# A blockwise scan with one exact iteration a block instead of two

## Chip, cores, metric

One core of a Trainium2 chip runs the kernel. The metric is the device time of one execution in microseconds (us); the times of the kernel before are the median of three runs and the profile of one more execution.

## What is computed

The input x is 2 sequences of 1024 rows of 128 numbers. Three residual layers follow each other: half a mixture of experts (a shared feed-forward layer and the best two of 8 experts), then a layer that learns while it reads, then half the same mixture again. The change is in the middle one:

```python
k, v = split(layernorm(x) @ W_KV)             # time first: 1024 steps, 2 rows each
def loss_fn(params, k_t, v_t):
    return mean((silu(k_t @ W1 + b1) @ W2 + b2 - v_t) ** 2)
def step(params, kvt):
    g = grad(loss_fn)(params, *kvt)
    return params - LR * g, None               # LR = 0.001, for each of W1, b1, W2, b2
params, _ = scan(step, (W1, b1, W2, b2), (k, v))
out = mlp(params, x @ W_Q)
```

So there are 1024 gradient steps, each on the parameters that the one before left.

## The kernel before, in words

The steps are taken in 16 blocks of 64 steps, 128 rows each (one row for each step and sequence). Within a block the activations of all 128 rows are guessed from the parameters at the block's start and the corrections that the earlier rows of the block make; the guess is put back in and the products are taken again. One such pass over a block is called an iteration here: h (`pe_first`, plus `pe_again`, L1050, which adds the correction by the old d), a silu and a tanh on ScalarE (ACT), y and the inner product a·a masked to earlier rows (`pe_y`, `pe_aa`, `dve_aa`, `pe_inner`), e on VectorE (DVE, `dve_e`), dA on TensorE (PE, `pe_da_old`, `pe_da`), the slope of silu on GpSimd (POOL, `pool_slope`) and d = slope times dA on DVE (`dve_d`). The rows of e and d then give the sums that move W1, b1, W2 and b2 (`pe_w1_sums` and its siblings, `moved_by` on DVE).

Two chains of iterations run side by side. The chain `ahead` is rounded: its operands are of type fp32r, and one product is one matmul record. The chain `final` is exact fp32, and one product is two records; a transposition is one in either. They have four banks of PSUM each, their own semaphores and their own copies of the parameters.

The scan is a loop of 16 turns, written out in full for each engine (the loops `for turn in range(NBLK)`). In turn t the exact chain does two iterations on block t (`late[0]` from the last rounded iteration, `late[1]` from `late[0]`), takes the sums and moves the exact parameters. The rounded chain meanwhile does two iterations (`early[0]`, `early[1]`) on block t+1; its parameters are the exact ones after block t-1 plus its own sums of block t. In the last turn there is no rounded chain. The order in which each engine issues these operations is laid down by hand in five loops (PE, ACT, DVE, POOL, and the helpers); every engine works its queue in order, and the semaphores release it.

POOL also measures how far the two exact iterations differ (`gap`, L1497), squares and adds that, and squares and adds the last iteration itself. After the last turn DVE reduces the sums (L1820), PE adds them over the partitions, and DVE compares with the tolerance TOL. The result is a flag: at 0 all engines run 1024 single steps instead (`If(ok == 0)`). In the profiled execution that branch was not run. The products for the queries x @ W_Q stand on PE before and behind the sum of the squares.

Of the kernel before, what the change touches and what calls it, by code (L numbers as in the profile page):

```python
# [42 lines left out]
ROUNDS = 2  # L43
# [12 lines left out]
TOL = 5e-5  # L56
# [6 lines left out]
class Chain:  # L63
# [39 lines left out]
    ee_mm: Any  # L103
# [7 lines left out]
class Step:  # L111
# [9 lines left out]
    inner: bool = True  # L121


def mk_macaron(nc, x, wq, wkv, w1, b1, w2, w2t, b2, router, experts, out):
# [20 lines left out]
    with ExitStack() as ctx:  # L145
# [6 lines left out]
        def sem(name):  # L152
# [110 lines left out]
        last_ed = sb("last_ed", [P, ROUNDS, 2, P])  # L263
        last_aa, last_ee = (sb(n, [P, 2, P]) for n in ("last_aa", "last_ee"))
        b1_half = sb("b1_half", [P, 1])
        gap, gap_sq, new_sq = (relu[:, n // 2, n % 2 * 2 * P:(n % 2 + 1) * 2 * P].rearrange("p (a d) -> p a d", d=P)
                               for n in range(3))
        squares = y_out[:, 0:4, :]
        slots_dram = [nc.dram_tensor(f"slots_dram{f}", (NT * P, ROW), F32) for f in range(2)]
        y_dram = nc.dram_tensor("y_dram", (TOPK * T, P), F32)  # L270
        norms = sb("norms", [P, 4])
        nrm = sb("nrm", [1, 4])
        good = sb("good", [1, 2])
# [68 lines left out]
        new_squared = sem("new_squared")  # L342
        gap_done = sem("gap_done")
# [29 lines left out]
        def chain_sems(name, own):  # L373
# [12 lines left out]
                      rows_done=None, ee_mm=None, **chain_sems("ahead", ()))  # L386
# [3 lines left out]
                      w2t_sb[:], b1_sb[:], b1_half[:], b2_sb[:], **chain_sems("final", ("rows_done", "ee_mm")))  # L390
# [579 lines left out]
        def pool_key_part(pool, part, g):  # L970
# [10 lines left out]
            elif part == 4:  # L981
# [5 lines left out]
        PARAMS = ("w1", "b1_half", "b1", "b2", "w2t", "w2", "ahead_w1", "ahead_b1_half", "ahead_b1", "ahead_b2",  # L987
                  "ahead_w2t", "ahead_w2")
        LAST_PARAMS = ("w1", "b1_half", "b1", "b2", "w2t", "w2")
# [26 lines left out]
        def turn_steps(turn):  # L1016
# [34 lines left out]
        def pe_again(pe, step):  # L1051
# [3 lines left out]
            mm(x.h_bank, old.chain.ed[:, old.to, 1, :], old.chain.kk[:, step.block, :], start=False)\  # L1055
# [36 lines left out]
        def pe_aa(pe, step, turn):  # L1092
# [4 lines left out]
            if x is final and step.m:  # L1097
                pe.wait_ge(x.ee_done, step.m)
            if x is final:
                wait_param(pe, step, turn, "b1")  # L1100
# [14 lines left out]

        def pe_y_old(pe, step):

            x, old = step.chain, step.old
            pe.wait_ge(x.ee_done, old.m + 1)
            pe.wait_ge(x.erows_done, old.n + 1)  # L1120
            mm(x.y_bank, x.ed[:, old.to, 0, :], x.aa[:, old.to, :], stop=False)
            pe.wait_ge(x.a_done, step.n + 1)

        def pe_y_last(pe, step):
            x = step.chain
            mm(x.y_bank, x.w2, x.a, start=False).then_inc(x.y_done, 1)
# [14 lines left out]
        def pe_da_old(pe, step):  # L1141
# [10 lines left out]
            if step.inner:  # L1152
                pe.wait_ge(x.guess_done, step.m + 1)
            else:
                pe.wait_ge(x.d_done, step.n)
# [11 lines left out]

        def pe_ee(pe, step):
            x = step.chain
            pe.wait_ge(x.e_done, step.n + 1)  # L1170
            nc.tensor.matmul(x.y_bank[:, 2 * P:3 * P], x.e, x.e, start=True, stop=True).then_inc(x.ee_mm, 1)
# [118 lines left out]
        def dve_ee(dve, step):  # L1290
            x = step.chain
            if x is ahead:
                dve.wait_ge(x.da_done, step.n + 1)
                ee = x.d_bank[:, 0:P]
            else:
                dve.wait_ge(x.ee_mm, step.m + 1)
                ee = x.y_bank[:, 2 * P:3 * P]
# [821 lines left out]
```

## Time and profile before

| | us |
|---|---|
| median of 3 runs | 485.08 (483.19 to 486.23) |
| the profiled execution's own time | 484.08 |
| its span, first to last instruction | 481.9 |
| PE busy in the span | 430.7 |
| DVE, ACT, POOL busy | 280.8, 245.1, 243.1 |

Busy is the time in which an engine has an instruction running by the profile; a weight load (PEld) overlaps the matmuls. The first feed-forward layer ends near 156 us, the first rounded iterations run to 178, the 16 turns to about 328, and the second feed-forward layer fills the rest. The granted clock (PEclk) is a share of 2.4 GHz: 0.50 is the level of 1.2 GHz.

### The profile page before, as it was taken

How to read it: one execution, taken by the hardware profiler on the slowest of the kernel's cores; microseconds unless marked ns; L12 is line 12 of the kernel's file. 1: busy time of each engine (PE TensorE's matmuls, PEld its weight loads, DVE VectorE, ACT ScalarE, POOL GpSimd, SP SyncE). 2: the span in 40 equal slices, each digit the busy share in tenths (PEclk: the TensorE clock that was granted, in tenths of full speed). 3: DMA queues.
4: the chain of work that ended last, by engine and by line, in shares of the span. 5: the costliest groups of instructions: out<-in, count | busy, mean ns of one | idle time of the engine just before them, and what ended most of it. 6: DMA issues, size and time to landing. Idle time of an engine off the chain costs nothing.

```text
span 481.9 us, 9866 instructions
## 1 busy us (share of the span) xinstructions
PE 430.7 (89%) x2875; PEld 356.0 (74%) x2875; DVE 280.8 (58%) x1031; ACT 245.1 (51%) x617; POOL 243.1 (50%) x369
## 2 busy tenths in 40 slices
PE   7899899999908989999999999999799799999940
PEld 5444699999903679899999989974644499999930
DVE  4945455555528646677777777754965245555514
ACT  3594355555410445556556565544696145555520
POOL 4367777545500344555555546552247777554530
PEclk9799999999957999999999999999989999999985
DMA  8981334100075200000000000000001417110028
GB/s 231 260 278 56 113 104 151 37 26 25 18 186 175 41 1 0 3 2 2 1 2 1 1 2 2 3 0 1 2 23 56 112 50 205 35 34 28 20 63 216
DMA packets 34513, 30.89 MB, mean 64 GB/s; under 512 B 3838, under 2 KB 30085, under 8 KB 34464
## 3 DMA queue, kind: packets, MB, share of 16 engines
q1 hardware_dynamic: 24608, 19.17, 14.7%
q0 software_dynamic: 4544, 8.47, 5.4%
q10 hardware_dynamic: 5312, 2.62, 2.1%
q8 instruction: 27, 0.44, 0.4%
q14 instruction: 22, 0.18, 0.1%
HBM read 15.55 MB, written 15.61 MB: 65 GB/s over the span
## 4 chain that ended last, share of the span: by engine, by line
PE 73%; DVE 8%; DMA 6%; POOL 4%; issue 4%; ACT 4%; ACTq 0%; SPq 0%; DVEq 0%; POOLq 0%
PE bank L1308 18%; PE bank L741 15%; PE bank L728 14%; POOL slots_dram L1435 3%; PE bank L599 3%; DMA stage<-y_dram 3%; PE bank L1101 2%; PE bank L689 2%; PE bank L716 2%; PE bank L1178 2%; DMA stage<-slots_dram 2%; PE bank L1139 1%; DVE stats L419 1%; PE bank L699 1%; PE bank L1162 1%
## 5 line engine op out<-in xcount | busy, mean ns | idle before, releaser
L1692 DVE TENSOR_TENSOR sq<-bank,relu 128x512 f32<-128x512 f32 x86 | 59.5, 692 | 84.2 <-ACT relu L839 84.0
L1440 POOL DMA_INDIRECT y_dram<-y_out,stage x78 | 76.9, 986 | 59.2 <-ACT y_out L865 52.6
L741 PE MATMUL bank<-proj_w,sq 128*128 x624 | 86.4, 281 | 2.8 <-DVE sq L1692 2.8
L728 PE MATMUL bank<-tileT,tile_w 128*128 128x128 f32 x624 | 83.2, 277 | 0.0
L1435 POOL DMA_INDIRECT slots_dram<-rows,slots x64 | 63.3, 990 | 35.0 <-DVE slots L535 15.2
L741 PEld LDWEIGHTS bank<-proj_w,sq 128*128 128x128 f32 x624 | 75.6, 191 | 6.5 <-issue 3.5
L839 ACT ACTIVATE relu<-bank 128x512 f32<-128x512 f32 x94 | 56.1, 596 | 45.4 <-PE bank L728 37.6
L728 PEld LDWEIGHTS bank<-tileT,tile_w 128*128 128x128 f32 x624 | 76.9, 195 | 0.0
L865 ACT ACTIVATE y_out<-bank,stage 128x128 f32<-128x128 f32 x78 | 28.7, 368 | 33.2 <-PE bank L741 33.2
L1303 POOL TENSOR_TENSOR sq<-sq,last_rows 128x128 f32<-128x128 f32 x32 | 14.7, 458 | 54.2 <-DVE sq L1279 54.2
L599 PE MATMUL bank<-ones 128*128 128x512 f32 x32 | 20.6, 790 | 15.4 <-DVE res L1743 12.6
L1710 DVE COPY tile_w<-fc_w 128x512 f32 x78 | 33.1, 426 | 0.0
L689 PE MATMUL bank<-ln_t,fc_w 128*128 128x512 f32 x64 | 32.8, 608 | 0.0
L599 PEld LDWEIGHTS bank<-ones 128*128 128x128 f32 x32 | 7.6, 251 | 23.8 <-DVE res L1743 12.8
L1303 POOL TENSOR_TENSOR sq<-sq,guess_rows 128x128 f32<-128x128 f32 x33 | 15.1, 457 | 13.2 <-DVE sq L1279 12.5
L689 PEld LDWEIGHTS bank<-ln_t,fc_w 128*128 128x128 f32 x64 | 11.9, 196 | 12.3 <-issue 12.3
L1256 ACT CAST ahead_ed<-bank 128x128 fp32r<-128x128 f32 x33 | 8.8, 267 | 22.8 <-PE bank L1178 22.8
L1241 ACT CAST guess_rows<-bank 128x256 fp32r<-128x256 f32 x33 | 12.4, 376 | 13.8 <-PE bank L1087 13.8
L1268 DVE SCALAR_TENSOR_TENSOR sq<-bank,b_sb,stage 128x128 f32<-128x128 f32 x32 | 11.2, 352 | 11.7 <-PE bank L1308 11.7
L1139 PE MATMUL bank<-ident,sq 128*128 128x128 f32 x65 | 17.9, 276 | 0.0
L975 POOL CAST rounded<-stage 128x512 fp32r<-128x512 f32 x4 | 2.5, 615 | 29.8 <-ACT stage L951 29.8
L1739 DVE TENSOR_TENSOR res<-res,stage 128x512 f32<-128x512 f32 x8 | 5.5, 688 | 20.0 <-DMA stage<-y_dram 20.0
(278 smaller groups left out, 1046.6 us busy)
## 6 DMA issues: line engine op xcount, KB each, us to landing
slots_dram<-pad SPq DMA_DIRECT2D x2, 2535.0 KB, 14.0
stage<-slots_dram SPq DMA_DIRECT2D x18, 260.0 KB, 4.4
fc_w<-experts SPq DMA_DIRECT2D x1, 2048.0 KB, 20.3
proj_w<-experts SPq DMA_DIRECT2D x1, 2048.0 KB, 24.0
stage<-y_dram SPq DMA_DIRECT2D x8, 256.0 KB, 5.5
stage<-y_dram ACTq DMA_DIRECT2D x8, 256.0 KB, 6.2
y_dram<-y_out,stage POOLq DMA_INDIRECT x78, 2.3
res<-x SPq DMA_DIRECT2D x4, 256.0 KB, 3.8
```

The source lines that it names most:

```text
L599: nc.tensor.matmul(bank[0][:], ones[:], ones[:].unsqueeze(1).to_broadcast([P, 4, P]), start=True, stop=True)
L689: nc.tensor.matmul(wide_of(i)[0][:], fc_w[:, 0, f_cols], ln_t[:, g * COLS:(g + 1) * COLS], start=True, stop=True).then_inc(fc_done, 1)
L728: last = nc.tensor.matmul(bank[i % 2][:, f_cols], tile_w[:, i % 2, f_cols], tileT[:, (f * NQ + tile_q(i)) % 2, tile_cols(i)], start=True, ...
L741: last = nc.tensor.matmul(bank[4 + i % 2][:, 0:P], sq[:, i % 2, f_cols], proj_w[:, k, f_cols], start=j == 0, stop=j == FJ - 1)
L839: nc.scalar.activation(wide_of(i)[1], wide_of(i)[0][:], ACT.Relu).then_inc(relu_done, 1)
L865: nc.scalar.mul(y_out[:, t % YBUFS, :], bank[4 + i % 2][:, 0:P], tiles[:, t, P + 1:P + 2])\
L1303: nc.gpsimd.tensor_tensor(x.slope, x.u, x.rows[:, 0:P].bitcast(F32), ALU.subtract).then_inc(x.slope_done, 1)
L1308: return nc.tensor.matmul(out_bank[:, 0:P], lhs_t, rhs, start=start, stop=stop, skip_group_check=not alone)
L1435: nc.gpsimd.indirect_dma_start(to, bass.IndirectOffsetOnAxis(slots[:, n:n + 1], 0), rows[:, k, b, :], None, bounds_check=limit, oob_is_err ...
L1440: nc.gpsimd.indirect_dma_start(y_dram.ap(), bass.IndirectOffsetOnAxis(tiles[:, t, P:P + 1].bitcast(U32), 0), y_out[:, t % YBUFS, :], None, ...
L1692: nc.vector.tensor_tensor(wide_of(i)[2], wide_of(i)[0][:], wide_of(i)[1], ALU.mult)\
L1710: nc.vector.tensor_copy(tile_w[:, t % 2, :].rearrange("p (a c) -> p a c", a=1), fc_w[:, expert_of(packed, stored_as(t)), :]).then_inc(tile ...
```

## The change

`late` becomes one iteration: the exact chain starts from the last rounded iteration, does one iteration and takes the sums. Its correction by the old d is now read as fp32 in both factors (two records). The check compares the exact iteration with the last rounded one, and uses the difference between the two rounded ones (`gap_of_steps`, `square_steps`, `add_steps`) to estimate the contraction. The orders of all engines are written anew, so are the places of the parameter updates (six single functions for each chain). PE gets three products of a rounded unit matrix with itself a turn, `pe_scan_busy`, whose output nothing reads. The diff, cut to its core:

```diff
-ROUNDS = 2
+KEPT = 2
-TOL = 5e-5
+TOL = 1e-4
+GAP_LIMIT = 3e-3
...
+        def pe_scan_busy():
+            nc.tensor.matmul(final.h_bank[:, 2 * P:3 * P], ident_r, ident_r, start=True, stop=True)
...
-            late, early = [], []
-            for r in range(ROUNDS):
-                late.append(Step(final, ROUNDS * turn + r, turn + r, turn, r, late[-1] if r else earlier, r == 0))
+            late, early = Step(final, turn, turn, turn, turn % KEPT, earlier), []
+            for r in range(AHEAD):
                 early.append(Step(ahead, n + r, n + r, turn + 1, 1 + turn % 2 if r else 0, early[-1] if r else None))
...
-            mm(x.h_bank, old.chain.ed[:, old.to, 1, :], old.chain.kk[:, step.block, :], start=False)\
+            mm(x.h_bank, as_kind(step, old.chain.ed[:, old.to, 1, :]), x.kk[:, step.block, :], start=False)\
...
-        def pe_ee(pe, step):
...
-            if x is final and turn:
-                if step.to == ROUNDS - 2:
-                    act.wait_ge(gap_made, turn)
-                elif step.to == ROUNDS - 1:
-                    act.wait_ge(new_squared, turn + 1)
+            if x is final and turn >= KEPT:
+                act.wait_ge(gap_made, turn - KEPT + 1)
+                act.wait_ge(new_squared, turn - KEPT + 2)
+            if x is ahead and step.to and turn >= 1:
+                act.wait_ge(gap_made, turn)
```

POOL's turn after the change (the three new functions, `gap_of_last` and the order):

```python
def gap_of_steps(turn):
    old, new = (0 if turn else 1), 1 + (turn + 1) % 2
    pool.wait_ge(ahead.d_done, FIRST_AHEAD + AHEAD * turn)
    nc.gpsimd.tensor_tensor(step_gap, ahead_ed[:, new, 1, :], ahead_ed[:, old, 1, :], ALU.subtract)   # 128x128
def square_steps(turn): ...                    # step_sq = step_gap * step_gap
def add_steps(turn): ...                       # squares[:, 4, :] += step_sq
def gap_of_last(turn):
    pool.wait_ge(final.erows_done, turn + 1)
    pool.wait_ge(final.d_done, turn + 1)
    nc.gpsimd.tensor_tensor(gap, last_ed[:, turn % KEPT], ahead_ed[:, 1 + (turn + 1) % 2], ALU.subtract)
# a turn
gap_of_steps; square_gap; square_steps; square_new; slope early[0]; add_steps;
slope late; slope early[1]; add_gap; gap_of_last; add_new
```

ACT's turn, and DVE's:

```python
# ACT
offset late; erows before[1]; silu late; offset, silu, tanh early[0]; tanh late; guess_rows early[0];
guess, rows late; erows early[0]; silu, tanh early[1]; erows late; guess_rows early[1]
# DVE
ahead: w1, b2, b1_half, b1, w2t, w2;  aa early[0]; aa late; u, e early[0]; u, e late; d, ee early[0];
d late; aa, u, e early[1]; w1, b2; d, ee early[1]; b1_half, w2t, b1, w2
```

PE's turn, each name standing for its `pe_` function:

```python
pe_first(pe, late, turn)
pe_again(pe, late)
if more: w1, b1, w2, w2t sums of before[1]
pe_offset(pe, late, turn); pe_old_guess(pe, late)
pe_first early[0]
pe_aa, pe_a_transposed, pe_y late
pe_offset, pe_yrows, pe_aa, pe_y, pe_th_transposed early[0]
pe_yrows, pe_th_transposed late
pe_inner early[0]
pe_scan_busy()
pe_inner(pe, late)
pe_scan_busy()
pe_da, pe_e_transposed early[0]
pe_da_old late
pe_first, pe_again early[1]
pe_da, pe_e_transposed late
pe_offset, pe_old_guess, pe_yrows, pe_aa, pe_y, pe_th_transposed early[1]
pe_w2_sums(pe, late)
pe_scan_busy()
pe_inner early[1]; pe_w1_sums late; pe_da_old early[1]; pe_w2t_sums late
pe_da early[1]; pe_b1_sums late; pe_e_transposed early[1]
```

After the last turn `norms` has five columns instead of four (the reduction reads 640 elements a partition), and the comparison on DVE takes four operations more, two of them linked one behind the other.

## Rows read from the trace of the kernel before

**Rows 1.** The page, busy time of each engine over the whole span.
```profile
PE 430.7 (89%) x2875; PEld 356.0 (74%) x2875; DVE 280.8 (58%) x1031; ACT 245.1 (51%) x617; POOL 243.1 (50%) x369
```

**Rows 2.** Stretches: length, then busy PE, PEld, DVE, ACT, POOL; PEclk, DMA, GB/s.
```profile
188.00:197.30 9.30, 9.20 (x70) 8.24 (x70) 6.53 (x30) 5.51 (x19) 4.87 (x10) 1.00 0.01 4
318.00:328.00 10.00, 8.42 (x54) 6.56 (x54) 4.66 (x21) 3.31 (x12) 5.91 (x10) 1.00 0.01 2
```

**Rows 3.** The chain that ended last, 186 to 200 us, shares by line.
```profile
by line: PE bank L1308 58.6%; PE bank L1101 7.0%; PE bank L1162 6.0%; PE bank L1207 5.6%; PE bank L1178 5.0%; PE bank L1139 4.7%; PE bank L1148 3.7%; PE bank L1087 2.9%; PE bank L1197 2.5%; PE bank L1134 2.3%; PE bank L1171 1.6%; issue 1.1%
```

**Rows 4.** The same chain in order of time, second feed-forward layer: start, length.
```profile
435.72 0.89 PE bank L741 x8
```

**Rows 5.** Timeline of a turn, rounded chain: start, us, engine, line, operation.
```profile
255.43 0.37 ACT L1222 ACTIVATE ahead_a<-bank,ahead_b 128x128 fp32r<-128x128 f32 x1
...
259.26 0.37 ACT L1222 ACTIVATE ahead_a<-bank,ahead_b 128x128 fp32r<-128x128 f32 x1
...
260.23 0.36 PE L1087 MATMUL bank<-w_ident,ahead_a 128*128 128x256 f32 x1
...
260.63 0.38 ACT L1241 CAST guess_rows<-bank 128x256 fp32r<-128x256 f32 x1 [0.45 <-PE bank L1087]
...
261.24 0.29 PE L1308 MATMUL bank<-ahead_aa,guess_rows 128*128 128x128 f32 x1
...
261.57 0.35 DVE L1268 SCALAR_TENSOR_TENSOR e_w2t<-bank,ahead_b,stage 128x128 fp32r<-128x128 f32 x1
...
262.00 0.36 PE L1162 MATMUL bank<-e_w2t 128*128 128x256 f32 x1
...
262.40 0.29 DVE L1287 SCALAR_TENSOR_TENSOR ahead_ed<-sq,bank 128x128 fp32r<-128x128 f32 x1
...
263.52 0.22 PE L1197 MATMUL bank<-guess_rows,ahead_ed 128*128 128x2 f32 x1
...
263.78 0.29 DVE L1631 SCALAR_TENSOR_TENSOR ahead_w<-bank,w_sb 128x128 fp32r<-128x128 f32 x1 [0.40 <-PE bank L1197]
...
264.72 0.37 ACT L1222 ACTIVATE ahead_a<-bank,ahead_b 128x128 fp32r<-128x128 f32 x1
```

**Rows 6.** POOL's groups by line: busy us, mean ns, idle before, releaser.
```profile
L1303 POOL TENSOR_TENSOR sq<-sq,guess_rows 128x128 f32<-128x128 f32 x33 | 15.1, 457 | 13.2 <-DVE sq L1279 12.5
...
L1471 POOL TENSOR_TENSOR y_out<-y_out,relu 128x256 f32<-128x256 f32 x16 | 11.7, 731 | 0.2
...
L1458 POOL TENSOR_TENSOR relu<-relu 128x256 f32<-128x256 f32 x16 | 9.8, 615 | 1.3
```

**Rows 7.** Stretches as in rows 2, before and in the first turn.
```profile
176.00:178.00 2.00, 0.98 (x9) 1.01 (x9) 1.18 (x6) 0.13 (x1) 1.59 (x3) 1.00 0.00 0
...
179.00:180.00 1.00, 1.00 (x6) 1.00 (x5) 0.00 (x0) 0.06 (x1) 0.00 (x0) 0.50 0.00 0
```

**Rows 8.** Timeline of the first turn, PE at the lower clock.
```profile
179.17 0.63 PE L1308 MATMUL bank<-w_sb,sq 128*128 128x128 f32 x2
...
182.09 0.39 PE L1308 MATMUL bank<-last_rows,ahead_ee 128*128 128x128 f32 x2
```

**Rows 9.** Timeline of the last turn, exact chain and POOL's end.
```profile
318.97 0.36 ACT L1222 ACTIVATE sq<-bank,b_sb 128x128 f32<-128x128 f32 x1
...
322.26 0.29 DVE L1287 SCALAR_TENSOR_TENSOR last_ed<-sq,bank 128x128 f32<-128x128 f32 x1 [0.58 <-PE bank L1308]
...
325.49 0.29 DVE L1287 SCALAR_TENSOR_TENSOR last_ed<-sq,bank 128x128 f32<-128x128 f32 x1 [0.64 <-POOL sq L1303]
...
325.93 0.73 POOL L1497 TENSOR_TENSOR relu<-last_ed 128x256 f32<-128x256 f32 x1 [0.54 <-DVE last_ed L1287]
...
328.80 0.73 POOL L1471 TENSOR_TENSOR y_out<-y_out,relu 128x256 f32<-128x256 f32 x1
...
329.56 0.69 DVE L1820 TENSOR_REDUCE norms<-y_out 128x4 f32<-128x512 f32 x1 [1.97 <-POOL y_out L1471]
```

More of the change, by code:

```diff
@@ L1096, in pe_aa @@
                 pe.wait_ge(x.e_done, step.n)
[L1097 to L1098 removed]
             if x is final:
+                if step.n:
+                    pe.wait_ge(x.e_done, step.n)
                 wait_param(pe, step, turn, "b1")
@@ L1466, in square_new @@
             def square_new(turn):
+                new = last_ed[:, (turn - 1) % KEPT]
                 nc.gpsimd.tensor_tensor(new_sq, new, new, ALU.mult).then_inc(new_squared, 1)
@@ L1482, in _ @@
                 late, early = turn_steps(turn)
+                gap_of_steps(turn)
                 if turn:
                     square_gap(turn)
-                    add_gap(turn)
-                pool_slope(pool, late[0])
+                square_steps(turn)
                 if turn:
@@ L1490, in _ @@
                     pool_slope(pool, early[0])
+                add_steps(turn)
+                pool_slope(pool, late)
+                if early:
+                    pool_slope(pool, early[1])
+                if turn:
+                    add_gap(turn)
+                gap_of_last(turn)
                 if turn:
                     add_new(turn)
-                for step in late[1:] + early[1:]:
-                    pool_slope(pool, step)
-                pool.wait_ge(final.erows_done, ROUNDS * (turn + 1))
-                pool.wait_ge(final.d_done, ROUNDS * (turn + 1))
-                nc.gpsimd.tensor_tensor(gap, new, last_ed[:, ROUNDS - 2], ALU.subtract).then_inc(gap_made, 1)
             for part in (square_gap, add_gap, square_new, add_new):
@@ L1535, in _ @@
                 late, early = turn_steps(turn)
+                act_offset(act, late, turn)
                 if before:
                     act_erows(act, before[1], turn - 1)
-                act_offset(act, late[0], turn)
-                act_silu(act, late[0], turn)
-                act_tanh(act, late[0], turn)
+                act_silu(act, late, turn)
                 if early:
@@ L1784, in _ @@
                 late, early = turn_steps(turn)
-                dve_aa(dve, late[0])
-                dve_u(dve, late[0])
-                dve_e(dve, late[0], turn)
+                more = early and turn
+                if more:
+                    dve_ahead_w1(turn - 1)
+                    dve_ahead_b2(turn - 1)
+                    dve_ahead_b1_half(turn - 1)
+                    dve_ahead_b1(turn - 1)
+                    dve_ahead_w2t(turn - 1)
+                    dve_ahead_w2(turn - 1)
                 if early:
                     dve_aa(dve, early[0])
+                dve_aa(dve, late)
+                if early:
                     dve_u(dve, early[0])
-                dve_d(dve, late[0])
-                if early:
                     dve_e(dve, early[0], turn)
-                dve_ee(dve, late[0])
+                dve_u(dve, late)
+                dve_e(dve, late, turn)
                 if early:
@@ L1797, in _ @@
                     dve_ee(dve, early[0])
-                dve_e(dve, late[1], turn)
-                dve_u(dve, late[1])
+                dve_d(dve, late)
                 if early:
                     dve_aa(dve, early[1])
-                dve_d(dve, late[1])
-                if early:
                     dve_u(dve, early[1])
                     dve_e(dve, early[1], turn)
-                more = turn < NBLK - 2
                 dve_w1(turn)
-                dve_b1(turn)
+                dve_b2(turn)
@@ L2029, in _ @@
             pe.wait_ge(norms_done, 1)
-            nc.tensor.matmul(bank[7][0:1, 0:4], ones[:, 0:1], norms[:], start=True, stop=True).then_inc(total_done, 1)
+            nc.tensor.matmul(bank[7][0:1, 0:5], ones[:, 0:1], norms[:], start=True, stop=True).then_inc(total_done, 1)
             pe_query_hidden(2).then_inc(qh_done, 1)
```

234 lines of the change are left out of this document (110 added, 124 removed).

## The prediction

> **What bounds the kernel now.** I began with the page: TensorE is busy 89% of the span and no other engine over 60% [rows 1]. A share over the whole span can't price a change in one stage, so next came the stretches. The turns of the scan run from about 178 to 328 us; in one turn (188.00 to 197.30) PE is busy 9.20 of 9.30 us and took 70 matmul records, 0.133 us each, while POOL is busy 4.87 [rows 2]. The reader is to see there that one turn is one period of 9.3 us: the first silu of the rounded chain starts at 255.43 and again at 264.72, so 9.29 us [rows 5]. Then the chain that ended last over a turn: its shares are PE's alone, 1.1% is issue [rows 3]. So before the change the turn is as long as PE's own queue, and no dependence between engines is late in it. What a pass costs when nothing is waited for: eight passes of the second stage take 0.89 us, 0.112 each [rows 4]. 70 passes at that price are 7.8 us and the four products 256 columns wide cost about another pass each (8.3 us in all); the other 1.0 us of the 9.29 is small waits at the head of PE's in-order queue.
>
> **The change, part by part.** I count passes by the code: an exact product has two matmul records, a rounded one or a transposition one. Before: first exact iteration 22, second 23, the two rounded iterations 9 and 12, sums of the rounded chain 4; together 70, as the records say [rows 2].
>
> Second exact iteration dropped: its products before the sums go (15 passes: h 2 and 2, y 2 and 2, three transpositions, dA 2 and 2). The sums stay, on the one iteration left. The product e·e of the first goes (2). The correction of h by the old d is now an exact product, since it reads both factors as exact ones (+1). Three unread rounded products (+3). Net -13: 57 passes. With them go 4 operations on ACT and 4 on DVE a turn.
>
> What ends the turn then? By PE alone: 57 x 0.112 plus four wide ones is 6.8 us, the lower end. By the old turn's mean with its waits, 57 x 0.133 = 7.6 us. The third answer is the chain that PE's queue used to cover: two rounded iterations, then sums and new weights, then the first silu again. I walked the new order along it, one queue per engine, with the durations of [rows 5] and about 0.03 us from PE to ACT or DVE and 0.06 back, the gaps seen between those rows. Bare iteration, silu to silu: silu 0.37, rows of y 0.36, their copy 0.38, inner product 0.29, e 0.35, dA 0.36, d 0.29, h again 0.30 (as the inner product), and 0.36 in hops, about 3.1 us. The old order took 3.83 (255.43 to 259.26), since exact products stood between.
>
> In the new order the first rounded iteration loses 0.15, because its y follows the exact chain's a·a, transposition and y on PE, and DVE's a·a mask waits for it: 3.24 us. The second, silu to the end of d, is 2.7 bare and 2.87 with the same kind of delay. From there to the next silu: the exact chain's h (four passes) and the four sums are first on PE, the bias sums end 0.71 after d, new w1 0.03 + 0.29, first product 0.06 + 0.31: 1.45 (old order: d ends 262.69, silu 264.72, 2.03). Sum 3.24 + 2.87 + 1.45 = 7.56 us. I take 7.56; PE's 6.8 fits under it with 0.75 to spare. Upper end: if iterations stay as slow as before (3.83, and 3.43 from silu to the end of d), 3.83 + 3.43 + 1.45 = 8.7 us.
>
> Does what is off that chain stay off it? The exact chain has one iteration where it had two; in the walk its d ends 2.3 us before the second rounded d, and its sums take gaps in PE's queue. ACT's bias of the exact offset now stands first in its queue and waits for the new b2, with the rounded e-rows copy and the exact silu behind it. In the walk b2 comes 0.3 us after the second rounded dA begins, offset and copy are done at 1.0, and PE reaches the sums that read the copy at 1.2: 0.1 to spare, and what b2 comes later than that goes 1:1 onto the chain. The exact inner product waits for ACT's exact guess, with the rounded dA queued behind it on PE: 0.2 us to spare. The unread products wait for nothing, 0.34 us in gaps, at most 0.34 on the path. The reordered parameter updates are the same operations. The waits added to the e-rows copies ask for gaps and squares of a turn or two back: nothing, up to the length of POOL's lag if that grew past a turn.
>
> POOL is the narrow one. It gains three operations of 0.457 and loses a slope: 4.87 us of a turn [rows 2] become 5.8. Between the second rounded slope and the next turn's first, seven operations stand in its queue: three of 0.73, two of 0.61, two of 0.457 [rows 6], 4.33 us by durations, some 4.0 start to start. Among them is the new gap operation, which waits for the exact d; the squares and the slopes are behind it, and d of the rounded chain waits for those. The walk wants the slope 4.0 us after the previous one: just hidden. If durations count in full, 0.3 us a turn comes onto the chain (7.9).
>
> Turns: fifteen have a rounded chain, 15 x (9.29 - 7.56) = 26.0 us, from 8.9 (8.7 a turn) to 37 (6.8).
>
> The last turn has the exact chain alone. Before, d of its first iteration starts at 322.26 and of its second at 325.49, 3.2 us apart [rows 9]. But the end is POOL's: five operations from 325.93 to the reduction at 329.56, and the flag behind it. In the walk POOL, still with the squares of the turn before, gets to the last addition 2.2 us earlier than now; the reduction reads 640 instead of 512 elements (0.69 now, +0.17, scaled); the two links added to the check (DVE) lie beside the query products. Gain 2.0, between 0 (should POOL be later) and 3.2. PE then waits some 1.5 us for the sums of squares, where it waited 0.5; a clock fall there would take back up to 2.
>
> Prologue and both feed-forward stages are untouched. Sum: 26.0 + 2.0 = 28 off. The profiled execution took 484.08 us (span 481.9 and 2.2 around it): 456. The median of the runs is 1.0 above that execution: 457.
>
> **The clock.** The granted clock is 1.00 over the turns, and it was 1.00 too from 318 to 328, where the exact chain runs alone in many small gaps and PE is busy 8.42 of 10 us [rows 2]. It was 0.50 at 179 to 180, after a stretch (176 to 178) with PE busy 0.98 of 2 us [rows 7]. The new turn has 57 passes in 7.56 us, 7.5 a us, as many as now. So I hold it at 2.4 GHz. The Trainium skill (TensorE: Matmul & The Clock Gate, "A second HAM failure mode: psum-queue depth-cycling") says that frequent small idles between groups of matmuls can make the clock swing between its two levels; the stretch 318 to 328 does not bear that out, and the time by that rule is the clock rival's below.
>
> **Rivals.** *Contention stays or POOL sets the turn.* For it: POOL's margin is nought and every queue is in order. Against: POOL is idle 4.4 of 9.3 us now [rows 2]. Turn 8.2 to 8.7: 15 x 0.85 + 2 = 15 off at the middle, 470.
>
> *PE's floor.* The chain turns out shorter than the walk, and PE's passes set the turn at 6.8: 37 + 3 off, 445. Against: the hops are measured.
>
> *The clock falls to 1.2 GHz in the turns* (the slower side). At that level 14 passes took 2.92 us (179.17 to 182.09), 0.21 each [rows 8]: 57 and four wide ones 12.8 us a turn, 15 x 3.5 = 53 more, 536. It decides from a third of the turns on (1.73 gained against 3.5 lost). For it: PE now waits on the chain in each turn. Against: same passes per us.
>
> *The single steps run.* One exact iteration instead of two; the flag sends all engines into 1024 single steps. An exact iteration takes about 3.6 us from silu to the end of d [rows 9], with sums and update some 4.5: over 4 ms more. The bounds are loosened along with it, and nothing in a trace tells the residues.
>
> *No gain.* Something I did not see holds the turn at 9.3: 483.
>
> **How the numbers follow.** Forecast (turn 7.1 to 8.2, 447 to 466 us) 0.72; contention or POOL 0.12; PE's floor 0.06; clock 0.05; single steps 0.03; no gain 0.02. The range 447 to 469 holds the first case and half of the second, about 8 in 10. One per cent, 4.9 us, is about what a measurement of this kernel can tell from no change. Faster by over 1% takes the first three, 0.90; same 0.02; slower 0.08.
>
> **What would show it.** 2,667 matmul records (208 fewer), 64 fewer operations on ACT, 32 more on POOL. First silus of the rounded chain 7.4 to 7.8 us apart; silu to silu within a turn near 3.2; in the chain that ended last DVE and ACT appear with PE. POOL's first slope without idle time before it says that POOL binds; a granted clock under 1.00 after 190 us says the clock does. I am wrong in kind if the period stays above 8.7, or if the chain is PE's alone again.

## The result and the profile after

The changed kernel takes 459.14 us (median of four runs, 458.50 to 461.08) where the kernel before took 484.91 beside it (four runs): ratio 0.9477, 95% interval 0.9435 to 0.9519. That is 25.8 us off; 28 were forecast. The profiled execution's span went from 481.9 to 456.9 us. The page of the kernel after, busy time of each engine, answers to [rows 1]:

```profile
PE 403.6 (88%) x2667; PEld 329.0 (72%) x2667; DVE 263.0 (58%) x971; ACT 227.4 (50%) x553; POOL 252.4 (55%) x401
```

The counts are those forecast: 208 matmul records and 64 operations on ACT fewer, 32 more on POOL. The shares hardly moved, so the page can't say what happened. The stretch that answers to the first of [rows 2], and the one in which PE now waits for the sums of squares (columns as there):

```profile
188.00:197.30 9.30, 9.30 (x72) 8.42 (x70) 6.31 (x30) 5.70 (x21) 6.12 (x12) 1.00 0.01 4
...
303.00:310.00 7.00, 5.43 (x17) 2.17 (x16) 1.98 (x9) 3.98 (x6) 1.41 (x3) 1.00 0.00 1
```

By this view PE is busy 9.30 of 9.30 us, more than before, and the clock is at 2.4 GHz. The chain that ended last, by line, as in [rows 3] but from 186 to 200 us of the kernel after, agrees with it:

```profile
by line: PE bank L1292 60.6%; PE bank L1096 6.7%; PE bank L1156 6.3%; PE bank L1110 5.8%; PE bank L1167 5.5%; PE bank L1136 4.4%; PE bank L1196 3.6%; PE bank L610 2.9%; PE bank L1186 2.4%; PE bank L1131 1.5%; PE bank L1145 0.4%
```

PE alone. By the prediction's own test ("wrong in kind ... if the chain is PE's alone again") this would make the passes the bound. The experiments below say otherwise. What does show the turn is the rounded chain in the timeline, one turn of the kernel after as in [rows 5] (start, us, engine, line, operation):

```profile
250.39 0.36 ACT L1211 ACTIVATE ahead_a<-bank,ahead_b 128x128 fp32r<-128x128 f32 x1
...
250.95 0.35 PE L1096 MATMUL bank<-w_ident,ahead_a 128*128 128x256 f32 x1
...
251.51 0.29 DVE L1250 SCALAR_TENSOR_TENSOR ahead_aa<-bank,nmask 128x128 fp32r<-128x128 f32 x1 [0.85 <-PE bank L1292]
...
251.86 0.33 PE L1292 MATMUL bank<-ahead_aa,guess_rows 128*128 128x128 f32 x1
...
252.28 0.46 POOL L1287 TENSOR_TENSOR sq<-sq,guess_rows 128x128 f32<-128x128 f32 x1 [0.20 <-DVE sq L1268]
...
252.64 0.38 PE L1156 MATMUL bank<-e_w2t 128*128 128x256 f32 x1
...
253.06 0.29 DVE L1276 SCALAR_TENSOR_TENSOR ahead_ed<-sq,bank 128x128 fp32r<-128x128 f32 x1
...
253.77 0.37 ACT L1211 ACTIVATE ahead_a<-bank,ahead_b 128x128 fp32r<-128x128 f32 x1 [0.33 <-PE bank L1292]
...
255.76 0.29 DVE L1632 SCALAR_TENSOR_TENSOR w_sb<-bank,w_sb 128x128 f32<-128x128 f32 x1
...
256.32 0.29 DVE L1276 SCALAR_TENSOR_TENSOR ahead_ed<-sq,bank 128x128 fp32r<-128x128 f32 x1
...
257.35 0.29 DVE L1632 SCALAR_TENSOR_TENSOR ahead_w<-bank,w_sb 128x128 fp32r<-128x128 f32 x1
...
258.13 0.36 ACT L1211 ACTIVATE ahead_a<-bank,ahead_b 128x128 fp32r<-128x128 f32 x1
```

Silu at 250.39, second silu at 253.77, d ends at 256.61, next silu at 258.13: 3.38 + 2.84 + 1.52 = 7.74 us a turn, against 3.83 + 3.43 + 2.03 = 9.29 before [rows 5]. The walk had 3.24 + 2.87 + 1.45 = 7.56. Eleven of the fourteen turns are within 0.01 of 7.74; three are longer by 0.07 to 0.28. Of POOL's two slopes, the first stands after 0.20 us of idle time. The exact chain does not hold the turn up here: its new W1 is done at 256.05 (255.76 + 0.29), and the rounded update that reads it (`ahead_w`) starts at 257.35.

The end of the scan, to be held against [rows 9]:

```profile
296.00 0.37 ACT L1211 ACTIVATE sq<-bank,b_sb 128x128 f32<-128x128 f32 x1 [0.36 <-PE bank L1292]
...
303.76 0.72 POOL L1474 TENSOR_TENSOR y_out<-y_out,relu 128x256 f32<-128x256 f32 x1
304.52 0.82 DVE L1838 TENSOR_REDUCE norms<-y_out 128x5 f32<-128x640 f32 x1 [2.90 <-POOL y_out L1474]
```

From the exact silu of the last turn to the reduction are 8.52 us, where it was 10.59 (318.97 to 329.56).

### The profile page after: what moved, and what is told of

It reads as the page before. It is cut to its first block, busy times and chain, and to the rows that moved or that the text cites. A ratio compares the mean times of both kernels' runs of the same rounds, so it can differ in the third digit from the quotient of the medians.

```text
span 456.9 us, 9332 instructions
## 1 busy us (share of the span) xinstructions
PE 403.6 (88%) x2667; PEld 329.0 (72%) x2667; DVE 263.0 (58%) x971; ACT 227.4 (50%) x553; POOL 252.4 (55%) x401
## 4 chain that ended last, share of the span: by engine, by line
PE 65%; DVE 7%; POOL 7%; DMA 7%; ACT 6%; issue 6%; ACTq 1%; DVEq 0%; SPq 0%; POOLq 0%
PE bank L751 16%; PE bank L738 15%; PE bank L1292 15%; POOL slots_dram L1419 4%; PE bank L604 3%; DMA stage<-y_dram 3%; PE bank L726 2%; DMA stage<-slots_dram 2%; ACT rows L802 2%; DVE stats L424 2%; PE bank L1096 2%; PE bank L1156 1%; ACT relu L849 1%; PE bank L1110 1%; PE bank L1167 1%
## 5 line engine op out<-in xcount | busy, mean ns | idle before, releaser
L699 PE MATMUL bank<-ln_t,fc_w 128*128 128x512 f32 x64 | 34.8, 642 | 0.0
L1250 DVE SCALAR_TENSOR_TENSOR ahead_aa<-bank,nmask 128x128 fp32r<-128x128 f32 x33 | 9.6, 291 | 20.7 <-PE bank L1292 20.7
L841 ACT COPY tileT<-bank 128x512 f32<-128x512 f32 (+1 forms) x20 | 11.5, 576 | 12.3 <-PE bank L726 11.2
L726 PE MATMUL bank<-ident,stage 128*128 128x128 f32 x78 | 12.7, 288 | 4.3 <-DMA stage<-slots_dram 4.3
L1204 ACT ACTIVATE last_offset<-stage,b_sb 128x128 fp32r<-128x128 f32 x16 | 6.4, 402 | 19.7 <-DVE b_sb L1632 19.7
```

The source lines that it names most:

```text
L699: nc.tensor.matmul(wide_of(i)[0][:], fc_w[:, 0, f_cols], ln_t[:, g * COLS:(g + 1) * COLS], start=True, stop=True).then_inc(fc_done, 1)
L726: last = nc.tensor.transpose(bank[6 + n % 2][:, tile_place(t)], tiles[:, t, 0:P], ident[:])
```

## The experiments

All ratios are to the kernel before on the same chip. Period is the distance of the rounded chain's first silus in a regular turn, split at its second silu; granted clock 1.00 over the turns unless said.

| kernel | us | ratio, 95% interval | period | split |
|---|---|---|---|---|
| before | 484 | 1 | 9.29 | 3.83 + 5.46 |
| after | 459.14 | 0.9477 (0.9435 to 0.9519) | 7.74 | 3.38 + 4.36 |
| e1 no unread products | 458.52 | 0.9467 (0.9439 to 0.9496) | 7.76 | 3.39 + 4.37 |
| e2 six of them | 460.72 | 0.9503 (0.9479 to 0.9527) | 7.82 | 3.45 + 4.37 |
| e3 small POOL operations | 458.97 | 0.9484 (0.9457 to 0.9511) | 7.74 | 3.38 + 4.36 |
| e4 two POOL operations more | 462.72 | 0.9552 (0.9520 to 0.9584) | 8.00 | 3.64 + 4.36 |
| e5 old orders | 497.67 | 1.0308 (1.0267 to 1.0349) | 8.99 at clock 1.00 | 3.83 + 5.16 |
| e11 old orders, products | 493.44 | 1.0198 (1.0172 to 1.0225) | 8.99 at clock 1.00 | 3.83 + 5.16 |
| e6 sums first | 458.15 | 0.9473 (0.9446 to 0.9500) | 7.70 | 3.38 + 4.33 |
| e8 rounded chain first | 467.32 | 0.9664 (0.9637 to 0.9691) | 8.34 | 4.12 + 4.22 |
| e9 the same, no products | 467.35 | 0.9660 (0.9632 to 0.9688) | 8.34 | 4.12 + 4.22 |
| e10 second order | 459.65 | 0.9493 (0.9468 to 0.9518) | 7.86 | 3.62 + 4.24 |
| e13 third order | 463.16 | 0.9572 (0.9545 to 0.9599) | 8.12 | 3.63 + 4.49 |
| e14 the same, no products | 461.91 | 0.9553 (0.9526 to 0.9579) | 8.01 | 3.52 + 4.49 |

**Is it PE's queue? (e1, e2)** The theory is that the rounded chain's latency sets the turn; the rival, which the chain of waits and the busy share speak for, that PE's passes do.

```diff
-                pe_scan_busy()     # all three calls taken out (e1)
+                pe_scan_busy()     # each call made twice (e2)
```

> The three unread products of a turn are left out, nothing else; the output is the same. PE's queue as the bound: 54 passes instead of 57, 0.33 to 0.41 us less in each of 16 turns, 5 to 6.5 us faster (period 7.74 to about 7.35). Chain through all engines as the bound (mine): the products stand in gaps in which PE waits for ACT's exact guess, for e and for the a-a mask, so the period stays between 7.6 and 7.74 and the time within 2 us. The clock as their use: without them the granted clock falls under 1.00 in the turns, and the period grows to 8 us or more.

> Each of the three unread products is issued twice, so six a turn. PE's queue as the bound: 0.33 us more in each of 16 turns, about 5 us slower (period about 8.1). Chain as the bound (mine): the second copy of the first and of the third fits into a wait, the second copy ahead of the rounded dA costs up to 0.1 us: period 7.74 to 7.85, 0 to 1.6 us slower.

The stretch of 100 us in the turns, first the kernel after:

```profile
188.00:288.00 100.00, 99.80 (x736) 90.46 (x734) 71.80 (x333) 56.10 (x194) 72.28 (x139) 1.00 0.01 2
```

and e1, without the products:

```profile
188.00:288.00 100.00, 98.24 (x695) 86.45 (x695) 72.02 (x333) 55.67 (x192) 72.22 (x139) 1.00 0.01 2
```

PE takes 41 records fewer in the 100 us and is busy 98.24 instead of 99.80: the busy time of the others stretches to fill the place. The period does not shorten (7.76 against 7.74). So the last 5% of PE's passes were in gaps that neither view shows, and the busy share of a pipelined PE does not say that PE binds. The Trainium skill warns of that measure (Perfetto Trace Analysis, "Identifying the Most-Contended Engine": matmul occupancy is no good measure of how close one is to the limit); it names the share of the peak rate reached and the busy share of the weight loads as better ones. Here the weight loads were busy 90 and 86% at the same period, so that share alone does not say what sets the turn either. Three products more cost 0.08 us in a regular turn and 0.10 on the mean of 14, not the 0.33 of a full queue. The cost lies in the first part (3.45 for 3.38), where a second copy now stands ahead of the rounded dA, as was expected. Nor does the clock in this order need the products: it is 1.00 without them.

**Is it POOL? (e3, e4)** e3 cuts the three new operations to two columns (the estimate of the contraction then reads almost nothing of the difference, and another column stands in for its sum); e4 adds two idle products of 128x128 ahead of the first slope.

```diff
-                nc.gpsimd.tensor_tensor(step_gap, ahead_ed[:, new, 1, :], ahead_ed[:, old, 1, :], ...)
+                nc.gpsimd.tensor_tensor(step_gap[:, 0:2], ahead_ed[:, new, 1, 0:2], ahead_ed[:, old, 1, 0:2], ...)
```
```diff
+                for spare in (spare_a, spare_b):
+                    nc.gpsimd.tensor_tensor(spare[:], ident[:], ident[:], ALU.mult)
                 if early:
                     pool_slope(pool, early[0])
```

> POOL's three added operations (difference of the two rounded iterations, its square, its sum) work on 2 of the 128 columns, and the comparison takes the first sum of squares in place of the fifth; so the estimate of the contraction is left out. That frees about 1 us of POOL in each turn. POOL as the bound of the turn: period down by 0.3 us or more, 5 us faster. Mine: POOL idles about 0.2 us before the first rounded slope now, and the slope ends 0.3 us before d wants it, so the period stays at 7.74; only the last turn, which ends with POOL's queue, gains: 0.5 to 1.5 us.

> POOL gets two more operations of 128x128 (0.41 us apart) before the first rounded slope of each turn, whose results nothing reads. POOL with room to spare (over 0.9 us): no change. POOL at its margin (mine): 0.2 us of idle time and 0.3 us before d wants the slope make 0.5 us; 0.82 us of work puts the chain 0.3 us later in each turn: period about 8.05, 4 to 6 us slower.

With POOL's work cut the period stays 7.74. What was expected of the last turn came too: from its exact silu to the reduction e3 takes 7.98 us instead of 8.52, so the end of the scan is POOL's. With two operations more, POOL in e4 runs into the slope without a pause:

```profile
253.88 0.41 POOL L1494 TENSOR_TENSOR spare_a<-ident 128x128 f32<-128x128 f32 x1
254.24 0.41 POOL L1494 TENSOR_TENSOR spare_b<-ident 128x128 f32<-128x128 f32 x1
254.59 0.47 POOL L1288 TENSOR_TENSOR sq<-sq,guess_rows 128x128 f32<-128x128 f32 x1
```

They take 0.71 us start to start, and silu to silu within the turn grows by 0.26: POOL had 0.45 us to spare. The time grew by 3.6 us, a little under the 4 to 6 expected. The kernel after shows the same sum: 0.20 idle before the slope, and the slope ends (252.74) 0.28 before dA does (253.02), 0.48 in all. "POOL's margin is nought" was too strict; "just hidden" was right.

**The fewer passes, or the new orders? (e5, e11)** e5 does the work of e1, in the orders in which the kernel before issued it on PE, ACT, DVE and POOL. Its core:

```diff
                 pe_first(pe, late, turn)
                 pe_again(pe, late)
-                if more: w1, b1, w2, w2t sums of before[1]
-                pe_offset, pe_old_guess late;  pe_first early[0];  ...
+                if more: w1, w2 sums;  pe_offset late;  b1, w2t sums;  pe_old_guess late
+                pe_aa, pe_a_transposed, pe_yrows late;  pe_first early[0];  pe_y, pe_th_transposed late
+                pe_offset, pe_aa early[0];  pe_inner late;  pe_y, pe_yrows early[0];  pe_da_old late;  ...
```

> The changed kernel's work (one exact iteration, the three new POOL operations, the longer check) issued in the orders of the kernel before on PE, ACT, DVE and POOL, without the three unread products; compared with the run that has the new orders and no unread products (458.52 us, turns 7.79 us apart). If the dropped passes alone made the gain, the rounded chain, which is the limit now, is as long here: turns 7.7 to 7.9 us apart, 457 to 461 us. If the newly laid orders made a part of it (the prediction's upper end, iterations as slow as in the old order), silu to silu within a turn stays near 3.8 us and the turns are 8.3 to 8.7 us apart: 14 x 0.5 to 0.9, so 465 to 472 us. I expect the middle, 8.1 us and 463.

This run was the surprise: 54 passes a turn instead of 70, and slower than before. Two things are in it. First the turn with the clock at 1.00, timeline of e5:

```profile
261.90 0.35 ACT L1211 ACTIVATE ahead_a<-bank,ahead_b 128x128 fp32r<-128x128 f32 x1
...
262.55 0.46 PE L1292 MATMUL bank<-last_aa,last_guess 128*128 128x128 f32 x2
...
262.90 0.33 PE L1096 MATMUL bank<-w_ident,ahead_a 128*128 128x256 f32 x1
...
263.79 0.30 PE L1292 MATMUL bank<-ahead_aa,guess_rows 128*128 128x128 f32 x1
...
265.71 0.37 ACT L1211 ACTIVATE ahead_a<-bank,ahead_b 128x128 fp32r<-128x128 f32 x1 [0.25 <-PE bank L1292]
...
268.55 0.29 DVE L1276 SCALAR_TENSOR_TENSOR ahead_ed<-sq,bank 128x128 fp32r<-128x128 f32 x1
...
269.92 0.29 DVE L1631 SCALAR_TENSOR_TENSOR ahead_w<-bank,w_sb 128x128 fp32r<-128x128 f32 x1 [0.40 <-PE bank L1186]
```

The next first silu is at 270.87. So 3.81 (3.83 in most turns) + 3.13 + 2.03: of the three parts of before, 3.83 + 3.43 + 2.03, only the middle one is shorter, by 0.30. Here is the first part as a stretch (columns as in [rows 2]), in the kernel before:

```profile
255.43:259.26 3.83, 3.83 (x31) 3.50 (x31) 2.70 (x10) 2.38 (x9) 2.17 (x4) 1.00 0.00 0
```

and in e5:

```profile
261.90:265.71 3.81, 3.17 (x20) 2.46 (x18) 2.54 (x10) 1.84 (x8) 2.58 (x5) 1.00 0.01 2
```

It is as long with 20 matmul records as with 31. So PE's passes are hardly what set its length before, though PE was busy all the time. In the old order the rows of y start 1.00 after the silu, behind the exact inner product, where they start 0.56 after it in the kernel after; the inner product follows 1.89 after the silu instead of 1.47; new W1 waits for b1's sums (L1186), which stand behind the w2 sums and the exact offset. So with the order kept, dropping 16 passes alone is worth 0.3 us a turn: a chain of 8.99 us lay under the 9.29. Whether PE's queue or the waits of the second exact iteration made the last 0.3 is not shown, since no unread products were added to the kernel before. The other 1.2 us a turn (8.99 to 7.76, same work) come from the orders.

Secondly the clock, the stretches of e5:

```profile
184.00:186.00 2.00, 1.45 (x10) 1.14 (x11) 0.58 (x2) 1.00 (x3) 0.14 (x1) 1.00 0.00 0
...
192.00:194.00 2.00, 1.58 (x10) 1.21 (x10) 0.49 (x2) 0.89 (x3) 0.89 (x2) 1.00 0.01 4
194.00:196.00 2.00, 1.68 (x10) 1.52 (x9) 1.16 (x4) 0.37 (x1) 1.14 (x2) 0.53 0.00 0
196.00:198.00 2.00, 2.00 (x12) 2.00 (x11) 1.30 (x8) 0.51 (x2) 0.79 (x2) 0.50 0.00 0
```

After stretches in which PE waits on the chain (busy 1.58 of 2.00 us) the clock falls to 0.50, the level of 1.2 GHz, and comes back in the next turn. Not each such stretch is followed by a fall: 184 to 186 is not. From one turn's second silu to the next turn's first it is then 7.8 us instead of 5.16, in full or in half in 8 of 14 turns. Over 100 us of turns the granted clock is 0.85. The Trainium skill describes such a swing for a kernel of another kind, with bf16 products of 512 columns (TensorE: Matmul & The Clock Gate, "A second HAM failure mode: psum-queue depth-cycling"): frequent short idles between groups of matmuls, and a clock that goes back and forth between its two levels. e5's trace agrees, with idles and both levels (1.00 and 0.50); e9's does not, with waits of PE in each turn (busy 1.54 to 2.00 us of 2.00) and 1.00 throughout.

Are the unread products what keeps it there? e11 puts them into e5's gaps:

```diff
                     pe_e_transposed(pe, late)
+                pe_scan_busy()
                     pe_da(pe, early[0])
...
                     pe_e_transposed(pe, early[0])
+                    pe_scan_busy()
                     pe_again(pe, early[1])
...
                     pe_th_transposed(pe, early[1])
+                    pe_scan_busy()
                     pe_da_old(pe, early[1])
```

> The run with the old orders (497.7 us, where the clock fell to a mean of 0.83 over the turns; turns 8.99 us apart where it stayed at 1.00) with the three unread products put back, each just ahead of a wait of PE (before the first rounded dA, before the correction of the second rounded h, before the second rounded dA by the old e). If unread products in the gaps keep the clock up, the granted clock is 1.00 over the turns, the turns are 9.0 to 9.1 us apart and the time is 476 to 480 us. If they are too few for it, the clock stays near 0.83 and the time at 493 to 500. In neither case does the time come under 470: the old orders themselves hold silu to silu within a turn at 3.83.

```profile
194.00:196.00 2.00, 1.55 (x9) 1.24 (x10) 0.52 (x3) 0.92 (x4) 1.10 (x3) 1.00 0.01 4
196.00:198.00 2.00, 1.74 (x11) 1.63 (x11) 1.05 (x4) 0.37 (x1) 0.95 (x2) 0.72 0.00 0
198.00:200.00 2.00, 2.00 (x12) 2.00 (x11) 1.30 (x8) 0.41 (x2) 0.87 (x3) 0.50 0.00 0
```

The same swing (these are e11's stretches), 0.84 over the turns. 493.44 against 497.67 us is a difference that the intervals bear out, but whether it is the products' doing is not shown: 7 turns of 14 are hit in its profile instead of 8. It is far from the 476 to 480 of a steady clock. Three products of some 0.11 us did not end the swing.

**Is there more in the order? (e6, e8, e9, e10, e13, e14)** If the chain's latency sets the turn, what stands ahead of it in the queues can be moved behind it. e6 moves one thing: the sums for W1 and b1 into a bank of their own, ahead of the exact correction.

```diff
                 pe_first(pe, late, turn)
-                pe_again(pe, late)
                 if more:
                     pe_w1_sums(pe, before[1], ahead_upd1)
                     pe_b1_sums(pe, before[1], ahead_upd1)
+                pe_again(pe, late)
+                if more:
```

> The sums of the rounded chain for W1 and b1 go to a bank of their own and are issued ahead of the exact chain's correction of h, so that they no longer stand behind its two passes and the mask of e.e. If the path d, sums of W1, new W1, first product, silu is what ends the turn, the silu comes 0.1 to 0.2 us earlier: turns 7.55 to 7.65 us apart, about 457. If the path over the new b2 and the offset, which ends at the same time, holds as well, nothing moves: 7.74 and 459, within 0.5 us. If PE's queue set the turn, nothing moves either.

0.03 us a turn. What holds the silu now shows in e6's timeline:

```profile
256.61 0.30 PE L1292 MATMUL bank<-rounded,ahead_w 128*128 128x128 f32 x1
...
256.72 0.40 ACT L1204 ACTIVATE ahead_offset<-stage,ahead_b 128x128 fp32r<-128x128 f32 x1
...
257.02 0.35 ACT L1211 ACTIVATE ahead_a<-bank,ahead_b 128x128 fp32r<-128x128 f32 x1
```

The first product ends at 256.91, but the silu stands in ACT's queue behind the rounded offset, which waited for the new rounded b2. In the kernel after the two paths end level: the product at 258.08, the silu 0.31 behind the start of the offset (257.82). e8 moves both, and keeps e6's bank.

```diff
 # PE
+first late; all four sums; first early[0]; again, offset, old_guess late;
+offset, yrows, aa, y early[0]; aa late; th early[0]; a_transposed late; inner early[0]; y, yrows, th late; ...
 # ACT
-silu late; offset, silu, tanh early[0]; tanh late; guess_rows early[0]
+offset, silu early[0]; silu late; tanh, guess_rows early[0]; tanh late
 # DVE, after d of early[1]
-ee; b1_half, w2t, b1, w2;  ahead: w1, b2, b1_half, b1, w2t, w2
+b1_half, b1, w2t; ahead w1; w2; ahead b2, b1_half, b1, w2t, w2; ee
```

> Same operations as in the changed kernel, in an order that puts the rounded chain first at the turn's end and start: all four of its sums ahead of the exact correction of h, its new parameters ahead of the exact W2 and the mask on DVE, its offset and silu ahead of the exact silu on ACT, its products ahead of the exact a.a, transposition and y on PE. If the rounded chain's latency sets the turn, the turn shortens by what the walk with the measured durations gives, 0.3 us: turns 7.4 to 7.5 us apart, 15 x 0.3 = 4.5 off, 454 us. If PE's queue sets it (57 passes, busy 99.8% by the view), the order changes nothing: 7.74 and 459. If the exact chain, now up to 0.7 us later in the turn with some 0.9 to spare, becomes the limit: 7.6 to 8.0 us, 457 to 463.

> The same order without the three unread products, 54 passes a turn. If the rounded chain's latency sets the turn, the products lie in gaps: within 0.05 us a turn of the run with them, 454 us. If PE's queue begins to be the limit once the chain is shorter, it gains up to 3 x 0.11 = 0.33 us a turn over the run with them, 450 us. If the clock needs the products once the turn is shorter, a granted clock under 1.00 after 190 us and over 470 us.

8.34 us a turn and 467 us are outside all that was expected. The part that was aimed at got shorter (4.22 instead of 4.36), the other longer (4.12 instead of 3.38). e8's timeline says where:

```profile
256.41 0.33 PE L1292 MATMUL bank<-ahead_aa,guess_rows 128*128 128x128 f32 x1
...
257.05 0.29 DVE L1250 SCALAR_TENSOR_TENSOR last_aa<-bank,nmask 128x128 f32<-128x128 f32 x1 [0.69 <-PE bank L1292]
...
257.26 0.28 DVE L1268 SCALAR_TENSOR_TENSOR sq<-guess_rows,bank 128x128 f32<-128x128 f32 x1
...
257.45 0.35 DVE L1257 SCALAR_TENSOR_TENSOR e_w2t<-bank,ahead_b,stage 128x128 fp32r<-128x128 f32 x1
```

The rounded inner product is done at 256.74, but DVE stands 0.69 us before the exact mask, whose product now comes late, with the rounded u (which POOL's slope waits for) and e queued behind it. So the first part grew by what stands ahead in DVE's queue, a wait for a product that the new order on PE had put late. The products again cost nothing (e9).

e10 moves u and e ahead of that mask, the exact e behind the rounded d, and dA ahead of the exact inner product.

```diff
 # DVE
-aa early[0]; aa late; u, e early[0]; u, e late; d, ee early[0]; d late
+aa, u, e early[0]; aa, u late; d, ee early[0]; e, d late
 # PE
-inner late; da, e_transposed early[0]; da_old late; first, again early[1]; da, e_transposed late; offset, old_guess early[1]
+da, e_transposed early[0]; first early[1]; inner, da_old late; again, offset, old_guess early[1]; da, e_transposed late
```

> The order of the run with the rounded chain first (467.3 us, turns 8.34 us apart, silu to silu within a turn 4.12), with what its trace names taken away: the first rounded u and e stand ahead of the exact mask on DVE, the exact e behind the rounded d, and on PE the first rounded dA stands ahead of the exact inner product. If the late u behind the exact mask was what lengthened that iteration, silu to silu within a turn falls from 4.12 to 3.3 and the rest stays 4.2: turns 7.5 us apart, 15 x 0.2 under the changed kernel, 455 to 456 us. If the exact chain, whose e now comes some 0.4 us later against the second rounded silu, binds instead, the turn stays at 7.7 to 8.2, 459 to 466.

3.62, not 3.3, and 7.86 us a turn, within the second case. In e10 the exact u now stands ahead of the rounded d, which waits for it:

```profile
253.14 0.34 PE L1156 MATMUL bank<-e_w2t 128*128 128x256 f32 x1
...
253.64 0.29 DVE L1268 SCALAR_TENSOR_TENSOR sq<-last_rows,bank 128x128 f32<-128x128 f32 x1 [0.40 <-ACT last_rows L1235]
...
253.84 0.28 DVE L1276 SCALAR_TENSOR_TENSOR ahead_ed<-sq,bank 128x128 fp32r<-128x128 f32 x1
```

dA ends at 253.48, d could start at 253.5 and starts at 253.84. e13 moves that too, and the second iteration's y ahead of the exact dA.

```diff
 # DVE
-aa, u late; d, ee early[0]; e, d late; aa, u early[1]
+aa late; d, ee early[0]; u, e late; aa early[1]; d late; u early[1]
 # ACT
-erows late; guess_rows early[1]
+guess_rows early[1]; erows late
 # PE
-da, e_transposed late; yrows, aa, y, th early[1]; w2 sums late; inner early[1]; w1 sums late; da_old early[1]
+yrows, aa, y early[1]; da, e_transposed late; th, inner early[1]; w1 sums late; da_old early[1]; w2 sums late
```

> The second order with the rounded chain first (459.65 us, turns 7.86 us apart, silu to silu within a turn 3.62), with what its trace names moved again: the first rounded d ahead of the exact u on DVE (it stood 0.33 us behind it), the second iteration's y ahead of the exact dA on PE, its a.a mask ahead of the exact d on DVE, its rows of y ahead of the exact e-rows on ACT, the exact W2 sums behind the second rounded inner product. If what stands ahead of the rounded chain in the queues is all that lengthens it, silu to silu within a turn falls to 3.3 and the rest stays 4.24: turns 7.5 to 7.6 us apart, 454 to 456 us. If the exact chain, pushed back once more, is now the limit, its sums make d of the second iteration late: turns 7.7 to 8.0 us, 459 to 464.

> The same order without the three unread products. If they lie in gaps there too, within 0.5 us of the run with them; if PE's queue is now the limit, up to 0.33 us a turn (5 us) faster; if the clock needs them, a granted clock under 1.00 after 190 us and over 470 us.

8.12 us a turn: longer than in either case expected (the time, 463, is within the second). Now d is on time in e13, but the exact inner product, which waits for its copy, one unread product and the exact old dA stand on PE in front of the correction of the second rounded h:

```profile
254.94 0.29 DVE L1276 SCALAR_TENSOR_TENSOR ahead_ed<-sq,bank 128x128 fp32r<-128x128 f32 x1 [0.28 <-PE bank L1156]
255.00 0.46 PE L1292 MATMUL bank<-last_aa,last_guess 128*128 128x128 f32 x2
...
255.36 0.44 PE L1292 MATMUL bank<-last_rows,ahead_ee 128*128 128x128 f32 x2
...
255.55 0.31 PE L1292 MATMUL bank<-rounded,ahead_ed 128*128 128x128 f32 x1
```

d ends at 255.23, its product starts at 255.55. The exact W2 sums, late as well, sit in the second part, 4.49: the second rounded e is done at 258.03 and its dA starts at 258.33, behind them. Here the products do cost 0.11 us a turn (e14 against e13): one of them stands in that queue. Three orders, three places of the same kind: each took one wait off the chain and made another. None is faster than the kernel after; e1 and e6 are equal to it within the intervals.

## Why the prediction was right, and where not

**Total.** 457 forecast, 459.14 measured, in the likeliest case and its range. Between the two profiled executions 25.0 us of span went; they are found here, from the starts of the same operations: 14 turns 131.26 to 108.80, so 22.5; from the 15th turn's first silu to the reduction 18.36 to 15.41, 2.9; the start of the scan to its first silu 1.2; the way from the reduction to the second stage -0.4; the stretches ahead of the scan and behind it, in which nothing was changed, -1.6 and +0.4. That the total came within 2 us is in part luck: the misses below, on the turn, the 15th turn and the check, were partly made good by a gain at the start that the sum did not have.

**The turn.** The walk's 7.56 was 0.18 too short: 0.14 of it in the first rounded iteration (3.38 for 3.24), 0.07 between d and silu, -0.03 in the second. The walk put 0.15 on a bare first iteration for what stands ahead of it. In the timeline the rows of y start 0.13 later than bare, behind exact products on PE, and the inner product waits 0.10 for the a·a mask. Over 14 turns the 0.18 is 2.5 us, the largest miss. The method held: of the four values for the turn (6.8, 7.56, 7.6, 8.7) two are close. 7.6, the old mean per pass, is the closer number, but by luck: e1 has 54 passes and the same period. The walk of the new order has the mechanism. The lower end of the range does not follow from its turn of 7.1: 15 x 2.19 + 2.0 is 35 off, 450 and not 447.

**What bounds the kernel before.** Here a step failed. "No dependence between engines is late in it" was read from a chain that is PE's alone. e5 shows a chain of 8.99 us right under the 9.29, and its first part as long with 20 records as with 31. The prediction had the old order's 3.83, 3.43 and 2.03 before it. That they add up to 9.29 proves nothing, since parts from one silu to the same silu a turn later always add up to the turn. What was missing is the walk of the old order with the second exact iteration taken out. The upper end of 8.7 came near this, but took the new 1.45 for granted in it. Had the orders not been changed, a forecast by passes alone would have been wrong by more than the whole gain (e5: 497.67 us).

**The 15th turn.** Counted as a full one (1.73). It leads into the last turn, which follows the exact chain, not the next rounded silu: its first silu to the last turn's exact silu went from 7.77 (311.20 to 318.97) to 6.89 (289.11 to 296.00), so 0.9.

**The last turn.** 2.0 forecast, 2.07 measured (10.59 to 8.52), by POOL's end as said; the reduction took 0.82 (0.86 forecast). The longer check was costed at nothing, beside the query products; from the reduction's start to the first residual it is 5.69 against 5.28, 0.4 us on the path, of which the longer reduction, which was counted, is 0.1. The clock did not fall while PE waited there (5.43 of 7 us busy, 1.00).

**ACT's bias and the exact guess.** Neither is late in the kernel after: the e-rows copy that "0.1 to spare" was about ends at 256.88, and PE reaches the sums that read it at 257.14. What the walk did not have is the rounded b2, whose path over the rounded offset ends level with the one over W1 (e6).

**Clock.** The rival did not come. The reason given, as many passes a microsecond as before, was not tested by itself: e5's turns have 54 passes in 9.0 us and swing, e14's 54 in 8.0 us and e9's 54 in 8.34 us do not, which would agree with it; but the stretch from 318 to 328 before had 54 in 10 us at 1.00 [rows 2], and all these kernels differ in their waits too. The price was of the right kind: some 2.6 us for a turn that is hit. What the sum missed is a gain: before, the clock was at 0.50 in the first turn [rows 7]; in the profile after it stays at 1.00 from 178 to 188 us. That is worth 0.9 us in that turn (10.19 before, 9.29 in a regular one), and some 0.4 of the 1.2 us up to the first silu: e5, with the old orders and the clock at 1.00, takes 2.50 us there, where it was 2.92 before and is 1.72 after, so the other 0.8 is the order's, which the sum did not have either. Without these 2.1 us the forecast would have been 4 us off instead of 2. Why the clock held there is open; it is not the unread products, since e1, e5 and e9 have none and hold 1.00 there.

**The other rivals.** PE's floor is refuted by e1 (three passes less, no gain), POOL as the bound by e3, contention by the period (7.74, not 8.2 to 8.7). The single steps did not run.

**The signs named.** Counts, period (7.4 to 7.8) and silu to silu (3.38, "near 3.2") were good signs. "DVE and ACT appear in the chain" was a bad one: where PE always has a record open, the view gives all time to PE, whatever set the pace.

## What to carry to other kernels

When one engine's queue fills a loop, walk the dependence chain in the present order as well, with the work that you mean to drop taken out: if it is nearly as long as the period, taking that work off the engine buys little until the order changes with it. Test a "full" TensorE by adding or removing a few passes that nothing reads; its busy share and the chain of waits can't tell a full queue from a chain hidden in it. With two chains in the same in-order queues, moving one instruction up can make the instruction behind it the next wait, as in all three orders here, so change an order with the timeline of the last one in hand, and measure each.

## What was not expected of the hardware

With the same products in another order the clock swings between 1.00 and 0.50 from turn to turn, and less work ran slower than before (1.0308). In e5 a stretch with PE busy 1.58 of 2 us came ahead of a fall and one with 1.45 did not, and three unread products a turn did not stop the swing, while e8's and e9's turns of 8.34 us, with waits of PE in each, kept 1.00. What decides between them is open.
